# A graph layer with linear attention on one core: the attention part in another order

## What is computed

```python
xn = layernorm(x)
x = x + gnn(xn, edges) + mix(xn)          # gnn: two graph convolutions; mix: two layers of the following
x = x + moe(layernorm(x))                 # 8 small experts, top 2

# one mix layer (8 heads of 64, M = 256 random features)
h = layernorm(x) * s + b
q, k, v = heads(h @ Wq + bq), heads(h @ Wk + bk), heads(h @ Wv + bv)
def features(t, is_query):
    dd   = (t * 64**-0.25) @ proj.T                                  # (nodes, 256)
    diag = 0.5 * sum(t * t, -1) * 64**-0.5
    stab = max(dd, -1) if is_query else max(dd, (-1, -2))            # a row's, or the whole head's
    return 256**-0.5 * (exp(dd - diag - stab) + 1e-4)
qp, kp = features(q, True), features(k, False)
ctx  = kp.T @ v                                                      # (256, 64) of each head
attn = (qp @ ctx) / (qp @ kp.sum(nodes))
x = x + attn @ Wo + bo
x = x + gelu(layernorm(x) @ W1 + b1) @ W2 + b2
```

## Time and profile before

| | us |
|---|---|
| three runs | 1353.6, 1357.81, 1362.41 (median 1357.81) |
| profiled execution: its own time | 1369.73 |
| profiled execution: span of its records | 1367.9 |
| TensorE busy | 1231.9 (90%) |
| VectorE busy | 838.8 (61%) |
| ScalarE, GpSimd busy | 317.0, 310.7 |
| attention of layer 0 | 130.9 to 275.8 |
| attention of layer 1 | 584.9 to 736.9 |

### The profile page before, as it was taken

One profiled execution on the slowest core, in us unless ns is written; L12 is line 12 of the kernel. 1 busy time (PEld: TensorE's weight loads), 2 busy tenths in 40 slices (PEclk: granted clock), 3 DMA queues, 4 the chain that ended last, 5 costly groups with the idle time before them and its releaser, 6 DMA issues.

```text
span 1367.9 us, 16675 instructions
## 1 busy us (share of the span) xinstructions
PE 1231.9 (90%) x5960; PEld 974.0 (71%) x5960; DVE 838.8 (61%) x1705; ACT 317.0 (23%) x592; POOL 310.7 (23%) x221
## 2 busy tenths in 40 slices
PE   4789798999999989889989999998888899899795
PEld 3667798978788867678988887885444588787432
DVE  6686477479844356736657896434777514617656
ACT  4246243123011014514332321000111112011202
POOL 3240102007431420020010382421000042400306
PEclk9988699799999999978869999999999999999887
DMA  5400000002210200000010031242000011001001
GB/s 192 154 1 1 31 1 32 0 1 79 77 62 6 96 19 1 1 31 1 1 32 1 16 123 46 62 166 92 0 1 0 8 32 32 31 1 29 1 0 62
DMA packets 15930, 52.12 MB, mean 38 GB/s; under 512 B 2640, under 2 KB 3472, under 8 KB 15216
## 3 DMA queue, kind: packets, MB, share of 16 engines
q1 hardware_dynamic: 12208, 40.23, 9.0%
q10 hardware_dynamic: 3648, 10.86, 2.2%
HBM read 44.80 MB, written 6.29 MB: 37 GB/s over the span
## 4 chain that ended last, share of the span: by engine, by line
PE 57%; DVE 23%; issue 15%; ACT 3%; POOL 2%; DMA 0%; POOLq 0%; ACTq 0%; DVEq 0%
PE ps_v L571 6%; PE ps_a L415 6%; PE ps_a L417 6%; PE ps_a L416 6%; PE ps_v L415 6%; PE ps_v L416 5%; PE ps_v L417 5%; PE ps_a L673 4%; DVE f_hi L1189 4%; PE ps_v L777 2%; DVE f_lo L1191 2%; PE ps_v L584 2%; PE ps_v L513 2%; DVE qmax L1358 2%; DVE expk L1312 2%
## 5 line engine op out<-in xcount | busy, mean ns | idle before, releaser
L415 PE MATMUL ps_a<-ht_hi,w_hi 128*128 128x512 f32 x496 | 196.7, 397 | 9.6 <-DVE headmask_r L1274 7.2
L416 PE MATMUL ps_a<-ht_lo,w_hi 128*128 128x512 f32 x496 | 195.6, 394 | 0.0
L417 PE MATMUL ps_a<-ht_hi,w_lo 128*128 128x512 f32 x496 | 195.6, 394 | 0.0
L1003 POOL TENSOR_TENSOR w_lo<-stage,w_hi 128x1024 fp32r<-128x1024 f32 x58 | 148.1, 2553 | 32.3 <-issue 28.0
L802 ACT ACTIVATE work<-ps_a,col_sb 128x512 f32<-128x512 f32 x96 | 66.7, 719 | 321.6 <-PE ps_a L417 207.6
L1001 POOL CAST w_hi<-stage 128x1024 fp32r<-128x1024 f32 x58 | 68.1, 1174 | 262.7 <-PE ps_a L417 162.1
L415 PEld LDWEIGHTS ps_a<-ht_hi,w_hi 128*128 128x128 f32 x496 | 94.2, 190 | 32.4 <-DVE headmask_r L1274 7.6
L1390 DVE TENSOR_TENSOR xm<-ps_v,xm 128x512 f32<-128x512 f32 x80 | 55.2, 690 | 94.2 <-PE ps_v L417 93.8
L417 PEld LDWEIGHTS ps_a<-ht_hi,w_lo 128*128 128x128 f32 x496 | 94.5, 190 | 20.2
L415 PE MATMUL ps_v<-w_hi,ht_hi 128*128 128x512 f32 x224 | 92.5, 413 | 18.1 <-issue 10.6
L416 PEld LDWEIGHTS ps_a<-ht_lo,w_hi 128*128 128x128 f32 x496 | 94.3, 190 | 19.6
(11 more groups left out here) (198 smaller groups left out, 2217.9 us busy)
## 6 DMA issues: line engine op xcount, KB each, us to landing
stage<-wstream SPq DMA_DIRECT2D x62, 512.0 KB, 3.6
xt_d<-xt_hi SPq DMA_DIRECT2D x2, 1024.0 KB, 5.0
xt_d<-xt_lo SPq DMA_DIRECT2D x1, 2048.0 KB, 11.4
ht_hi<-xt_d ACTq DMA_DIRECT2D x1, 2048.0 KB, 9.5
ht_lo<-xt_d ACTq DMA_DIRECT2D x1, 2048.0 KB, 15.3
x_again<-x ACTq DMA_DIRECT2D x8, 256.0 KB, 4.0
out<-xm SPq DMA_DIRECT2D x8, 256.0 KB, 2.0
rows_sb<-rows ACTq DMA_DIRECT2D x2, 768.0 KB, 4.7
```

Of the source, the lines that this page charges most:

```text
L415: nc.tensor.matmul(ps, left[0], right[0], start=first, stop=False)
L416: nc.tensor.matmul(ps, left[0], right[1], start=False, stop=False)
L417: return nc.tensor.matmul(ps, left[1], right[0], start=False, stop=last)
L1003: nc.gpsimd.tensor_tensor(lo, stage[:, j, :], hi.bitcast(f32), ALU.subtract).then_inc(w_split, 1)
```

## The change

Four edits go together. In a step, the query scores come first. The key scores of the next pair come in two halves, of four banks each, in steps 0 and 1. The contexts of a pair come in its third step, ahead of the first outputs that use them. For that, `expk` has two homes, used in turn: "nat" and "ht", the latter the place of the transposed hidden state, free during attention. ScalarE's exponentials of pair p + 1 move to steps 2 and 3 of pair p and step 0 of pair p + 1; VectorE asks for their bias behind the query scores of step 2; the last norms are turned behind the first half of the first key scores. The exponentials of pair 0, the work of each job, and the number of instructions stay as they are.

```diff
@@ attention_order, ddk_jobs, ring_v_attention
-        if s == 0 and g < STEPS:
-            yield "ctx", pair
-            if pair + 1 < NH // 2:
-                yield "ddk", pair + 1
         if g < STEPS:
             yield "ddq", g
+            if s < 2 and pair + 1 < NH // 2:
+                yield "ddk", g
+        if s == 2 and g < STEPS:
+            yield "ctx", pair
         if 1 <= g <= STEPS:
             yield "tr", g - 1
         if g >= 2:
             yield "at", g - 2
-def ddk_jobs(pair):
-    return [("ddk", pair, s, j) for s in range(NT // 2) for j in range(2)]
+def ddk_jobs(pair, tiles=range(NT // 2)):
+    return [("ddk", pair, s, j) for s in tiles for j in range(2)]
+def ddk_ahead(g):
+    pair, s = divmod(g, NT // 2)
+    return pair + 1, range(2 * s, 2 * s + 2)
         if what == "ddk":
-            yield from ddk_jobs(g)
+            yield from ddk_jobs(*ddk_ahead(g))
+            if g == 0:
+                yield "turned", 3
         elif what != "ddq":
             yield from ((what, g, j) for j in range(2))
-            if (what, g) == ("ctx", 0):
-                yield "turned", 3
@@ buffers
-        expk = at("expk", [P, 2, NT, M], f32, "nat")
+        expk = [at(f"expk{n}", [P, 2, NT, M], f32, region) for n, region in enumerate(("nat", "ht"))]
@@ TensorE
                     if what == "ddk":
-                        ddk(g)
+                        ddk(*ddk_ahead(g))
+                        if g == 0:
+                            turn_norms(3)
                     elif what == "ddq":
+                        if s == 0:
+                            written_a(("q", pair, H - 1))
                         scores(qS, pair, s, [bank("a", ("ddq", g, j)) for j in range(2)], a_full)
                     else:
-                        if what == "ctx":
-                            written_a(("q", g, H - 1))
...
-                        if (what, g) == ("ctx", 0):
-                            turn_norms(3)
@@ ScalarE, behind the query exponentials of step g, half j
-                        if s and pair + 1 < NH // 2:
-                            part_ = 2 * (s - 1) + j
-                            exp_k(pair + 1, (2 * NT * part_ + 5) // 6, (2 * NT * (part_ + 1) + 5) // 6)
+                        part_ = 2 * ((s + 2) % 4) + j
+                        if part_ < 6 and NT // 2 <= g + 2 <= STEPS + 1 and g + 2 < 4 * (NH // 2):
+                            exp_k((g + 2) // 4, (2 * NT * part_ + 5) // 6, (2 * NT * (part_ + 1) + 5) // 6)
@@ VectorE
+                    if NT // 2 - 1 not in tiles:
+                        return
                     dve.wait_ge(v_empty, v0 + done(MIX_V[("ddk", pair, NT // 2 - 1, 1)]))
                     nc.vector.tensor_reduce(kmax1[:, pair, :], kmax[:, pair, :, :], axis=AX.X,
                                             op=ALU.max).then_inc(kmax_ready, 1)
...
-                        ddk(g)
+                        ddk(*ddk_ahead(g))
+                        if g == 0:
+                            take_turned(3)
                         continue
...
-                    if (what, g) == ("ctx", 0):
-                        take_turned(3)
-                    if what == "ddq" and s == 0 and pair + 1 < NH // 2:
+                    if what == "ddq" and s == 2 and pair + 1 < NH // 2:
                         k_bias(pair + 1)
```

More of the change, by code:

```diff
@@ L517, in scores, with ddk @@
                                 last.then_inc(full, 1)
-                def ddk(pair):
-                    for s in range(NT // 2):
+                def ddk(pair, tiles=range(NT // 2)):
+                    for s in tiles:
                         scores(kS, pair, s, [bank("v", ("ddk", pair, s, j)) for j in range(2)], v_full)
@@ L570, in mix_layer @@
                                     for t in range(NT):
-                                        nc.tensor.matmul(context, expk[:, j, t, nodes(m)], V[:, t, g, of_head],
+                                        nc.tensor.matmul(context, expk[g % 2][:, j, t, nodes(m)], V[:, t, g, of_head],
                                                          start=t == 0, stop=False)
@@ L856, in exp_k @@
                         j, t = divmod(n, NT)
-                        nc.scalar.activation(expk[:, j, t, :], expk[:, j, t, :], ACT.Exp, scale=DN,
+                        nc.scalar.activation(expk[pair % 2][:, j, t, :], expk[pair % 2][:, j, t, :], ACT.Exp, scale=DN,
                                              bias=kbias[:, pair, j, t:t + 1]).then_inc(expk_done, 1)
@@ L1306, in low_parts, with ddk @@
                     last.then_inc(a_empty, 1)
-                def ddk(pair):
-                    for s in range(NT // 2):
+                def ddk(pair, tiles=range(NT // 2)):
+                    for s in tiles:
                         for j in range(2):
                             ps = job("ddk", pair, s, j)
-                            nc.vector.tensor_scalar(expk[:, j, 2 * s:2 * s + 2, :],
+                            nc.vector.tensor_scalar(expk[pair % 2][:, j, 2 * s:2 * s + 2, :],
                                                     ps.rearrange("p (t m) -> p t m", m=M), 1.0, -3.0e38, ALU.mult, ALU.max,
                                                     accum_out=kmax[:, pair, j, s:s + 1]).then_inc(v_empty, 1)
+                    if NT // 2 - 1 not in tiles:
+                        return
                     dve.wait_ge(v_empty, v0 + done(MIX_V[("ddk", pair, NT // 2 - 1, 1)]))
```

## The result

Four runs of the changed kernel took 1307.59, 1316.04, 1332.99 and 1336.76 us, median 1324.51, against a median of 1355.7 for the kernel before beside it. The ratio is 0.967, 95% interval 0.958 to 0.976: faster, with 1306 forecast and 1289 to 1333 as the range. Medians in this document are over all runs, while a ratio compares only the executions of each kernel within about 1.5% of its fastest, so the two can differ: here the medians alone would give 0.977. Measured once more on another occasion the changed kernel had 1315.48 (1307.77 to 1326.52, six runs) beside 1360.43, by medians 0.967, ratio 0.978 (0.968 to 0.988). Both kernels are uneven: the changed one spread over 29 and 19 us on these two occasions, the one before over 22 to 45 us where 11 or 17 runs of it were made.

The account below looks back on a forecast made before the run. TensorE bounds the kernel, VectorE second; attention loses to idling and low clock. Per layer 28.7 + 30.5 + 29.3 + 22.0 + 4.5 = 115.0, plus 5 clock, 120; 57 us off the profiled run, 52 off the 1357.8 median: 1306, range 1289 to 1333.

Parts of the forecast that it names:

- the stall: TensorE's 4.58 us idle before the second transposes, while the key all-reduce is awaited; to be hidden behind context 0, twice.
- the 1.6 us that were added: First pair: allowance for VectorE's query bias contending with GpSimd's subtractions; bounds 0 to 4.6 us.
- A layer without a fall: One layer's attention with no drop of the clock: 115.0 us, summed over the pairs and the drain.
- those 14.5: VectorE's time in us for a pair's first two steps, 6.65 each, plus 0.16 for the maximum and 0.6 for a wait.
- The third pair's stall: TensorE's 2.84 us idle in the third pair, put down to GpSimd's subtractions; taken as gone, bounds 0 to 4 us.
- An even chance of a slow context 0: Each layer: a new 2.4 us TensorE gap just ahead of context 0 lowers the clock there with even chance.
- The price of 11 us: Cost of a slow context 0: 7.4 for the context, 2.6 for transposes and outputs, 1 until recovery.
- Pairs 1 to 3 have no idle ahead of their contexts: Later pairs of each layer: no TensorE gap before contexts, so no clock fall was costed there.
- rival A: Full-bank gaps in key-score steps keep the clock falling ahead of two or more contexts a layer: 137 us, total 1335; chance 0.12.
- At the full clock the order brings nothing: Pair 1: 30.5 us forecast, 0.9 longer than the 29.6 before, as VectorE still has nothing to do during contexts.
- B: Key halves waiting for VectorE's banks hold transposes and contexts in TensorE's queue: slower, layer 159 us, total 1379; chance 0.05.
- C: Only the stall is hidden, 4.6 us twice; low-clock stretches move without shortening: 1348 us; chance 0.07.

Follow-up runs that it names:

- e1: Kernel before, with VectorE asking for the key bias behind the query scores of step 1, not step 0: 1356.32 us beside 1360.43, ratio 1.008.
- e5: Kernel before, with the weight split of load(3) behind the all-reduce of pair 1, not ahead of it: 1384.2 us beside 1358.68, ratio 1.024.
- e3: Changed kernel with unread score products filling TensorE's gaps in attention: 1312.0 us, ratio 0.975.
- e4: Changed kernel with the weight split of load(3) behind the all-reduce of pair 1, not ahead of it: 1315.15 us, ratio 0.975.
- e2: Changed kernel, nothing altered, run again as yardstick: 1315.48 us (1307.8 to 1326.5).
- e6: Kernel before, old order and stall kept, with unread score products filling TensorE's gaps: 1322.64 us beside 1358.68, ratio 0.978.
- e8: Changed kernel with both unread products in the gaps and the load(3) split behind the all-reduce of pair 1: 1312.0 us beside 1365.36, ratio 0.965.
- filled v3: Changed kernel with next key scores half in step 1, half between step 2's contexts, later bias and exponentials, plus unread products in gaps: 1305.52 us, ratio 0.972.

## Why the prediction was right
The time fell in the range, and the mechanism is the one forecast: the stall is hidden behind a context and low stretches go. The middle was missed. Attention took 256.2 us in the profiled execution where 240 was expected: 5.7 of the 16.2 too many are the order at full clock (117.8 for 115.0, twice), 10.5 are clock (20.5 for 10). That the first median (1324.51) is in the range at all owes something to chance: of its four runs one lay outside it (1336.76) and one at its edge (1332.99).
- **Place and price of the first pair.** From the first query score (133.64) to context 0 (145.41) are 11.77 us; "query scores 2 end at +11.8" was the forecast. VectorE enters step 4 at +28.86 (28.7). Two query biases took 1.57 and 0.35 us instead of 0.16 each, the 1.6 us that were added.
- **The stall is hidden, not gone.** VectorE waits 4.48 us beside contexts, as forecast. That a step without a context does not cover it is shown by e1 and e5.
- **A layer without a fall:** 115.0 forecast, 117.8 measured (e3, and e4 at 0.99). Part of the difference is in the steps with key scores: 7.7 us each, 15.4 for two where 14.5 was put down. The terms given for those 14.5 add up to 14.1 with one wait of 0.6 us and to 14.7 with two; the wait measured is about 1.1 in each step.
- **The third pair's stall** left with its cause, as forecast: contexts 2 to 3 take 22.9 us at 1.00 (layer 0), with no TensorE gap over 0.21 us.
- **Clock.** An even chance of a slow context 0 in each layer: one of two in the profiled execution (slow in layer 1, full in layer 0), with the same gap ahead of both; in that of e2 both ran full but for the first quarter in layer 0. The price of 11 us was about right: attention 137.7 with two falls is 19.9 over 117.8, some 10 each. One sentence was wrong: "Pairs 1 to 3 have no idle ahead of their contexts". The gap of 1.4 us in steps with key scores can be enough: the stretch at 644.2 begins behind one and goes through context 2, and in e2 context 1 of layer 1 was slow behind another. This is the mechanism of rival A, and layer 1, with contexts 0 and 2 slow, took 137.7 us where A had 137; layer 0 had no slow context. It is the part of the missed middle that is clock; that it also explains the medians, 9 and 18 us above 1306, fits but rests on two profiled executions.
- **Shares.** "The gain is only the stall and the clock" holds in the main: 28.3 of 40.7 us in attention are clock. "At the full clock the order brings nothing" holds for pair 1 (31.2 against 29.6 us). The 6.2 us a layer fit pair 0 and the third pair's stall: in e6 the four pairs of layer 0 take 32.5, 29.6, 33.8 and 28.4 us, so the first and third are 2.9 and 4.2 longer than the second, and the new order gives back some of the sum in its steps with key scores.
- **The shared port.** The Trainium skill (SBUF — State Buffer, "Who interferes with whom") counts operations with two SBUF inputs, and `tensor_scalar` in a two-port mode, among those that contend; the rows agree for operations with two SBUF inputs (2.57 us for 0.68, 1.57 for 0.16) and show two `tensor_scalar` of 128 x 8 held as well (2.52 us for 0.37), each beside a GpSimd subtraction; in which mode the latter ran no row shows.
- Rivals B and C fell: no run of the changed kernel was over 1336.8 (B had 1379, C 1348), and low stretches shrank from 119 to 51 us.

## What to carry to other kernels
Before an order of jobs is judged, keep TensorE busy through its gaps with products that nobody reads: the time then shows the order, and the difference to the plain run is what the clock costs. Do not put small products (here the contexts, 65 columns wide, beside which weight loads are busy 16.86 of 17.00 us in the earlier trace rows) behind a wait. A fall into a context cost some 10 us; behind gaps of 2.48 and 2.68 us with score products next it lasted 3.4 us or did not come (e8). A long wait is not safe there either: the old 4.58 us stall, ahead of transposes, had a low stretch of 10.2 us behind it. And when a wait is moved, ask what the queue behind it holds: on GpSimd the pause went to the next all-reduce, on VectorE the split met small operations.

## Not expected of the hardware
- An all-reduce on GpSimd starts 0.2 us after its input when GpSimd's work before it was an all-reduce, and 6 to 7 us after when a weight split lies between (6.0 before, 6.1 in e5, 6.9 in the changed kernel; e4 shows the same move as e5). The other way round it is the same: GpSimd idles some 7 us before the first subtraction of a split (7.13 in the earlier trace rows, 7.57 in e5), and before the second not. What GpSimd does in this time no run shows; the word "reload" in the expectations is a guess.
- The clock fell after gaps of only 1.4 us, and in layer 1 of the kernel before no gap but this one stood in the 9 us ahead of the low stretch at 661.0:

```profile
658.24 1.97 PE L571 MATMUL ps_v<-v_sb,expk 128*128 128x65 f32 x16 [0.82 <-ACT work L888]
```

- Once low in a context step it mostly stays so to the step's end (20.5 and 23.9 us), though TensorE is busy all the time; in e2 it rose once after 3 us. With no gap over 0.6 us in attention (e3) both layers ran at 1.00. Most gaps are not followed by a fall, though, and what decides it is open.
- Executions of one binary differ by 19 to 45 us where six or more were made. Filling the gaps brings this to 6 to 9 us (e6, e3, e8; 14 in the filled v3, where a gap of 2.7 us is left). The one unfilled kernel with a small spread (6 us) is e5, whose six runs all had a granted clock of 0.92. Where the clock falls differs, with the same gaps, from layer to layer and execution to execution.
